# A mixture-of-experts block on one core: the moving operand of the expert matmuls read in strides of 16-byte lines

## The chip, the cores and the metric

The kernel runs on one core of a Trainium2 chip. Its time is the device time of one execution, in microseconds (us). Two executions of the kernel before were timed, at 1880.53 and 1886.04 us; their median is 1883.28 us. One further execution was profiled, and everything below about where the time goes is read from that one.

## The reference, cut to what matters

The input has 8 groups of 1024 tokens, 256 values each. A gated recurrence runs first (three 256 x 256 projections, a sigmoid, a scan over the tokens), then a layer norm, a top-2 router over 8 experts, and the experts:

```python
# per expert E (8), group G (8), slot C (256), width M = 256, hidden H = 1368
expert_inputs = einsum('GSEC,GSM->EGCM', dispatch, x)
layer_w0 = einsum('EGCM,EMH->EGCH', expert_inputs, w0_kernel)
layer_w1 = einsum('EGCM,EMH->EGCH', expert_inputs, w1_kernel)
hidden = gelu(layer_w0) * layer_w1
expert_outputs = einsum('EGCH,EHM->EGCM', hidden, wo_kernel)
out = einsum('EGCM,GSEC->GSM', expert_outputs, combine)
```

Everything is float32. Each of the 8 experts has 8 x 256 = 2048 slots, and the hidden width 1368 is ten chunks of 128 and one of 88.

## The kernel before

Two parts follow each other. The first (the functions under `pipeline`) takes the 8 groups through the projections, the recurrence and the router, and scatters token rows into slots in HBM. The second (the functions under `experts`) is what the change touches; it loops over 8 experts, over 4 tiles `t` of 512 slots and over 11 chunks `hc` of hidden units.

For one chunk of one tile TensorE does two things:

- `up_chunk` (matmul at L1186): for w0 and w1 it multiplies 128 weight columns (the stationary operand, a slice of `whi` or `wlo`) by the tile's tokens (the moving operand, 512 columns of `xThi` or `xTlo`). Float32 accuracy comes from splitting each operand into a high and a low part and adding three of the four products (`PARTS`), over two halves `k` of the width: 2 x 3 x 2 = 12 matmuls of 512 columns, into the PSUM banks `up[hc % 2]`.
- `down_chunk` (matmul at L1202), two chunks behind: 128 tokens of the hidden values (`hhi` or `hlo`, now the stationary operand) by the 256 columns of wo for this chunk (columns 512 to 767 of `whi[:, hc]` or `wlo[:, hc]`, the moving operand), for four groups `j` of tokens and three products: 12 matmuls of 256 columns, into the banks `yb`, which collect over all 11 chunks.

Every matmul has a stationary operand of its own, so each is preceded by a weight load (LDWEIGHTS, engine PEld in the profile), which runs while the matmul before it streams its columns. The order on TensorE is written out by hand: up 0, up 1, up 2, down 0, up 3, down 1, ..., up 10, down 8, down 9, down 10. After up 6 stand eight 128 x 128 transposes (L1125) that prepare the next tile's tokens. The last chunk has 88 hidden units: before, its up matmuls load 88 stationary columns (`n`) and write 88 partitions, and its down matmuls have 88 rows.

ScalarE applies the gelu and rounds to the high part (L732, L738), VectorE multiplies and takes the low part (L1011, L1014). In tile 3 of an expert ScalarE and VectorE also split the next expert's weights (L723 and L1000), chunk by chunk as the down matmuls have finished with the old ones.

In SBUF, one float32 takes 4 bytes of each partition, so 4 columns are one line of 16 bytes, and 128 columns (512 bytes) are 32 lines. The buffers are laid out with paddings to multiples of 128 columns plus or minus one line: `xThi` and `xTlo` begin at a multiple of 128 columns, row `hc` of `whi` is 772 columns long and so begins `hc` lines behind such a multiple, and the same row of `wlo` one line earlier than that.

```python
whi = sb("whi", [P, HC, WROW], F32R)[:, :, 0:WCOL]
sb("between", [P, -(HC * WROW + 4) % P])
wlo = sb("wlo", [P, HC, WROW], F32R)[:, :, 0:WCOL]
```

Of the kernel before, what the change touches and what calls it, by code (L numbers as in the profile page):

```python
# [26 lines left out]
P = 128  # L27
# [42 lines left out]
class Chain:  # L70
# [14 lines left out]

    def end(self):
        assert self.n == self.per, (self.n, self.per)


def build(nc, x_in, w_qkva, gamma_in, router_in, w0_in, w1_in, wo_in, out):  # L90
    G, S, D = x_in.shape
    E, _, H = w0_in.shape
    CAP = (2 * S // E + 3) // 4 * 4
    KD = D // P
# [4 lines left out]
    HC = -(-H // P)  # L99
    HLAST = H - (HC - 1) * P  # L100
# [8 lines left out]
    WCOL = 2 * KD * P + D  # L109
# [10 lines left out]
    with ExitStack() as ctx:  # L120
        def sb(name, shape, dt=F32):
            return ctx.enter_context(nc.sbuf_tensor(name, shape, dt))

        def sem(name):
            return ctx.enter_context(nc.semaphore(name))
# [7 lines left out]
        xThi = sb("xThi", [P, 2, KD, T], F32R)  # L133
        xTlo = sb("xTlo", [P, 2, KD, T], F32R)
# [8 lines left out]
# [3 lines that stand above are left out]
# [64 lines left out]
        up = [bank[2:4], bank[5:7]]  # L210
        yb = [bank[4], bank[7]]
# [33 lines left out]
        back = sem("back")  # L245
# [786 lines left out]
        def _(pe):  # L1032
# [80 lines left out]
            for k in range(KD):  # L1113
                for c in range(NCH):
                    last = pe.transpose(bank[2 + 2 * k + c // 4][:, (c % 4) * P:(c % 4 + 1) * P],
                                        wraw[:, c, k * P:(k + 1) * P], ident[:, :])
# [52 lines left out]

            def up_chunk(e, t, hc):  # L1170

                n = P if hc < HC - 1 else HLAST
                c = HC * t + hc
                if t == 0:

                    wait(pe, w_split, e, HC, hc + 1)
                if hc == 0:
                    wait(pe, fx_lo, e, KD * FT, KD * (t + 1))

                user = c - 2 if hc >= 2 else c - hc - HC + max(q for q in range(HC) if q % 2 == hc)  # L1180
                wait(pe, mul_done, e, HC * FT, user + 1 + FREE_MUL)
                for w, done in ((0, up0), (1, up1)):
                    for m, (wp, xp) in enumerate(PARTS):
                        for k in range(KD):
                            at = (w * KD + k) * P
                            last = pe.matmul(up[hc % 2][w][0:n, :], (whi, wlo)[wp][:, hc, at:at + n],  # L1186
                                             (xThi, xTlo)[xp][:, t % 2, k, :],
                                             start=m == 0 and k == 0, stop=m == 2 and k == KD - 1)
                    last.then_inc(done, 1)

            def down_chunk(e, t, hc):

                n = P if hc < HC - 1 else HLAST
                wait(pe, h_lo, e, HC * FT, HC * t + hc + 1)
                if hc == 0:

                    wait(pe, y_read, e, FT * FJ, FJ * t + FJ)
                    pe.wait_ge(routed, G)
                for j in range(FJ):
                    for m, (wp, xp) in enumerate(PARTS):  # L1200

                        last = pe.matmul(yb[j // 2][:, (j % 2) * D:(j % 2 + 1) * D],  # L1202
                                         (hhi, hlo)[xp][0:n, hc % 3, j * P:(j + 1) * P],
                                         (whi, wlo)[wp][0:n, hc, 2 * KD * P:WCOL],
                                         start=hc == 0 and m == 0 and j % 2 == 0,
                                         stop=hc == HC - 1 and m == 2, skip_group_check=True)
                last.then_inc(down, 1)
# [36 lines left out]
```

## Time and profile before

| | us |
|---|---|
| median of the two timed executions | 1883.28 |
| the profiled execution | 1893.51 |
| its span, first to last instruction | 1891.6 |
| of the span, the first part, before the first expert matmul | 332 |
| from the first expert matmul to the last one's end | 1538.9 |
| TensorE busy with matmuls | 1779.5 |
| TensorE weight loads | 1531.4 |
| VectorE busy | 833.3 |
| ScalarE busy | 723.4 |

The profiled execution took 0.5% more than the median. A matmul's duration in the trace is longer than the distance to the next one's start, because matmuls are pipelined; what counts for the time is that distance from start to start, called the pitch below. The timeline merges neighbouring instructions of one kind ("x2"), so the pitch is the difference of two start times divided by the number of matmuls between them. The peak rate is one column per cycle of TensorE's 2.4 GHz clock, which would be 213.3 ns for 512 columns and 106.7 ns for 256.

### The profile page before, as it was taken

Reading aid. Unit: us, or ns where it says so; the run is one execution under the profiler, and the core shown is the slowest. Engines: PE = TensorE matmul, PEld = TensorE weight load, DVE = VectorE, ACT = ScalarE, POOL = GpSimd, SP = SyncE. Lnnn points to the kernel's source line nnn. Section 1 sums busy time; section 2 is a strip of 40 time slices with the busy share of each in tenths; the row PEclk is TensorE's granted clock in tenths of the full one; section 3 lists DMA queues with packets and bytes.
Section 4 is the critical chain, followed back from the end, with each engine's and each line's share of the span. In section 5 each row is a group of like instructions: output and inputs, shape, how many; then the busy total and the mean of one; then the engine's idle time right before and its main releaser. Section 6 shows DMA issues by size and latency. Waiting matters only on the chain.

```text
span 1891.6 us, 28176 instructions
## 1 busy us (share of the span) xinstructions
PE 1779.5 (94%) x10284; PEld 1531.4 (81%) x10284; DVE 833.3 (44%) x1672; ACT 723.4 (38%) x1242; POOL 394.7 (21%) x309
## 2 busy tenths in 40 slices
PE   5988885899999999999999999999999999999995
PEld 4776765688888888888888888888888888888884
DVE  5886764333443344334533353335333533353331
ACT  4554442233343334333433343335333533353331
POOL 3365556411111111111111111111111111111111
PEclk9988885799999999999999999999999999999998
DMA  9345423111321132113311231123112411142222
GB/s 315 116 170 191 152 96 124 57 23 23 82 54 23 23 81 55 23 23 70 66 23 23 66 70 23 23 59 77 23 23 49 87 23 23 40 95 49 75 67 56
DMA packets 113037, 129.76 MB, mean 69 GB/s; under 512 B 14552, under 2 KB 100504, under 8 KB 112792
## 3 DMA queue, kind: packets, MB, share of 16 engines
q1 hardware_dynamic: 88344, 94.21, 16.5%
q0 software_dynamic: 24576, 33.83, 10.5%
q8 instruction: 93, 1.52, 0.3%
q14 instruction: 24, 0.20, 0.0%
HBM read 68.23 MB, written 68.16 MB: 72 GB/s over the span
## 4 chain that ended last, share of the span: by engine, by line
PE 83%; DVE 4%; issue 4%; ACT 3%; POOL 3%; another core or an unknown queue 1%; DMA 1%; SPq 0%; ACTq 0%; DVEq 0%; POOLq 0%
PE bank L1186 52%; PE bank L1202 26%; POOL slots L549 2%; PE bank L1125 2%; PE bank L1050 1%; ACT xn L623 1%; DVE y L811 1%; ACT rows L639 1%; DVE st L832 1%; PE bank L1095 0%; DVE wlo L1000 0%; POOL sums L600 0%; DVE xTlo L803 0%; POOL pw L532 0%
## 5 line engine op out<-in xcount | busy, mean ns | idle before, releaser
L1011 DVE TENSOR_TENSOR y<-bank,sig 128x512 f32<-128x512 f32 (+1 forms) x352 | 243.2, 691 | 637.3 <-PE bank L1186 625.5
L600 POOL DMA_INDIRECT sums<-xring x128 | 207.5, 1621 | 1309.6 <-ACT xring L752 1196.3
L1186 PE MATMUL bank<-xThi,whi 128*128 128x512 f32 (+1 forms) x1408 | 445.8, 398 | 13.7 <-DVE wlo L1000 10.0
L1186 PE MATMUL bank<-xTlo,whi 128*128 128x512 f32 (+1 forms) x1408 | 443.9, 396 | 1.4 <-issue 1.4
L1186 PE MATMUL bank<-xThi,wlo 128*128 128x512 f32 (+1 forms) x1408 | 443.3, 396 | 1.5 <-issue 1.5
L738 ACT ACTIVATE hhi<-y 128x512 fp32r<-128x512 f32 (+1 forms) x352 | 222.5, 632 | 554.2 <-DVE y L1011 550.0
L1202 PE MATMUL bank<-whi,hhi 128*128 128x256 f32 (+1 forms) x1408 | 397.7, 282 | 0.0
L1202 PE MATMUL bank<-wlo,hhi 128*128 128x256 f32 (+1 forms) x1408 | 395.3, 281 | 1.5 <-issue 1.5
L1202 PE MATMUL bank<-whi,hlo 128*128 128x256 f32 (+1 forms) x1408 | 395.1, 281 | 1.5 <-issue 1.5
L1014 DVE TENSOR_TENSOR hlo<-y,hhi 128x512 fp32r<-128x512 f32 (+1 forms) x352 | 243.7, 692 | 246.3 <-ACT hhi L738 246.3
L732 ACT ACTIVATE sig<-bank 128x512 f32<-128x512 f32 (+1 forms) x352 | 210.4, 598 | 317.9 <-PE bank L1186 310.7
L1186 PEld LDWEIGHTS bank<-xThi,wlo 128*128 128x128 f32 (+1 forms) x1408 | 262.2, 186 | 70.1 <-issue 3.0
L1186 PEld LDWEIGHTS bank<-xTlo,whi 128*128 128x128 f32 (+1 forms) x1408 | 262.0, 186 | 68.7 <-issue 1.5
L1186 PEld LDWEIGHTS bank<-xThi,whi 128*128 128x128 f32 (+1 forms) x1408 | 243.6, 187 | 56.1 <-issue 17.6
L1202 PEld LDWEIGHTS bank<-whi,hhi 128*128 128x128 f32 (+1 forms) x1408 | 265.0, 188 | 12.8 <-issue 0.4
L1202 PEld LDWEIGHTS bank<-whi,hlo 128*128 128x128 f32 (+1 forms) x1408 | 264.9, 188 | 11.5 <-issue 0.4
L1202 PEld LDWEIGHTS bank<-wlo,hhi 128*128 128x128 f32 (+1 forms) x1408 | 265.3, 188 | 2.6 <-issue 2.6
L549 POOL DMA_INDIRECT slots<-rows,sloti x128 | 124.8, 975 | 87.0 <-DVE rows L918 45.4
L1000 DVE TENSOR_TENSOR wlo<-stage,whi 128x768 fp32r<-128x768 f32 x77 | 72.5, 956 | 33.7 <-ACT whi L723 31.8
L1050 PE MATMUL bank<-xThi,wThi 128*128 128x512 f32 x192 | 71.5, 456 | 14.1 <-DVE y L811 11.3
L752 ACT ACTIVATE xring<-bank,gslot 128x256 f32<-128x256 f32 x128 | 50.0, 473 | 73.8 <-PE bank L1202 73.8
L723 ACT ACTIVATE whi<-stage 128x768 fp32r<-128x768 f32 x77 | 63.7, 836 | 32.6 <-DMA stage<-in_L_ffn_wo_kernel 29.0
(109 smaller groups left out, 1096.7 us busy)
## 6 DMA issues: line engine op xcount, KB each, us to landing
stage<-in_L_ffn_w_kernel SPq DMA_DIRECT2D x160, 128.0 KB, 2.8
slots<-fill SPq DMA_DIRECT2D x32, 520.0 KB
xring<-slots SPq DMA_DIRECT2D x32, 520.0 KB
stage<-in_L_ffn_wo_kernel SPq DMA_DIRECT2D x80, 128.0 KB, 2.9
xring<-in_L_attn_x SPq DMA_DIRECT2D x16, 512.0 KB
sums<-xring SPq DMA_DIRECT2D x16, 512.0 KB
slots<-rows,sloti POOLq DMA_INDIRECT x128
sums<-xring POOLq DMA_INDIRECT x128, 3.8
```

The costliest lines, as they stand in the source:

```text
L549: pool.indirect_dma_start(slots[:, :], bass.IndirectOffsetOnAxis(sloti[:, g.parity, k, t:t + 1], 0), rows[:, g.parity, t, :], None).then_i ...
L600: pool.indirect_dma_start(sums[:, :], bass.IndirectOffsetOnAxis(idx, 0), ysb[:, t % 2, j, :], None, compute_op=ALU.add).then_inc(added, 16)
L723: act.activation(whi[:, hc, :], stage[:, hc % STAGES, :], ACT.Copy).then_inc(w_hi, 1)
L732: act.activation(gel[0:n, hc % 2, :], up[hc % 2][0][0:n, :], ACT.Gelu_apprx_tanh).then_inc(gelu_done, 1)
L738: act.activation(hhi[0:n, hc % 3, :], hf[0:n, hc % 2, :], ACT.Copy).then_inc(h_hi, 1)
L752: act.activation(ysb[:, t % 2, j, :], yb[j // 2][:, (j % 2) * D:(j % 2 + 1) * D], ACT.Copy, scale=gslot[:, t % 2, j:j + 1]).then_inc(y_rea ...
L1000: dve.tensor_tensor(wlo[:, hc, :], stage[:, hc % STAGES, :], whi[:, hc, :].bitcast(F32), ALU.subtract).then_inc(w_split, 1)
L1011: dve.tensor_tensor(hf[0:n, hc % 2, :], up[hc % 2][1][0:n, :], gel[0:n, hc % 2, :], ALU.mult).then_inc(mul_done, 1)
L1014: dve.tensor_tensor(hlo[0:n, hc % 3, :], hf[0:n, hc % 2, :], hhi[0:n, hc % 3, :].bitcast(F32), ALU.subtract).then_inc(h_lo, 1)
L1050: last = pe.matmul(dst[:, :], (wThi, wTlo)[wp][:, k, cols], (xThi, xTlo)[xp][:, h, k, :], start=m == 0 and k == 0, stop=m == 2 and k == KD ...
L1186: last = pe.matmul(up[hc % 2][w][0:n, :], (whi, wlo)[wp][:, hc, at:at + n], (xThi, xTlo)[xp][:, t % 2, k, :], start=m == 0 and k == 0, sto ...
L1202: last = pe.matmul(yb[j // 2][:, (j % 2) * D:(j % 2 + 1) * D], (hhi, hlo)[xp][0:n, hc % 3, j * P:(j + 1) * P], (whi, wlo)[wp][0:n, hc, 2 * ...
```

## The change

All expert matmuls read the columns of their moving operand in another order and write the columns of their result in the same other order, so that every result still lands where it did. The columns are taken in lines of four. With "every4" a matmul reads lines 0, 4, 8, ... to the end, then 1, 5, 9, ..., then 2, 6, ..., then 3, 7, ...; "every8" and "every16" do the same in steps of 8 and 16 lines; "every4 back" goes through each of its four passes from the end; "swapped" reads lines 1, 0, 3, 2, 5, 4, .... Which order is used depends on the tile `t` alone. In the up matmuls of the last chunk all 128 stationary columns are loaded and all 128 partitions are written; the 40 further ones hold columns that nobody reads the result of.

```diff
+def reordered(ap, order):
+
+    if order == "every4":
+        return ap.rearrange("p (i q c) -> p q i c", q=4, c=4)
+    if order == "every4 back":
+        return ap.rearrange("p (i q c) -> p q i c", q=4, c=4)[:, :, ::-1, :]
+    if order == "every8":
+        return ap.rearrange("p (i q c) -> p q i c", q=8, c=4)
+    if order == "every16":
+        return ap.rearrange("p (i q c) -> p q i c", q=16, c=4)
+    assert order == "swapped"
+    return ap.rearrange("p (i q c) -> p i q c", q=2, c=4)[:, :, ::-1, :]
+
+
+UP_ORDER = ("every4", "every8", "every4 back", "every16")
+DOWN_ORDER = ("every4", "every8", "every4 back", "swapped")
...
             def up_chunk(e, t, hc):
 
-                n = P if hc < HC - 1 else HLAST
...
-                            last = pe.matmul(up[hc % 2][w][0:n, :], (whi, wlo)[wp][:, hc, at:at + n],
-                                             (xThi, xTlo)[xp][:, t % 2, k, :],
+                            last = pe.matmul(reordered(up[hc % 2][w][:, :], UP_ORDER[t]),
+                                             (whi, wlo)[wp][:, hc, at:at + P],
+                                             reordered((xThi, xTlo)[xp][:, t % 2, k, :], UP_ORDER[t]),
                                              start=m == 0 and k == 0, stop=m == 2 and k == KD - 1)
...
-                        last = pe.matmul(yb[j // 2][:, (j % 2) * D:(j % 2 + 1) * D],
+                        last = pe.matmul(reordered(yb[j // 2][:, (j % 2) * D:(j % 2 + 1) * D], DOWN_ORDER[t]),
                                          (hhi, hlo)[xp][0:n, hc % 3, j * P:(j + 1) * P],
-                                         (whi, wlo)[wp][0:n, hc, 2 * KD * P:WCOL],
+                                         reordered((whi, wlo)[wp][0:n, hc, 2 * KD * P:WCOL], DOWN_ORDER[t]),
```

No instruction is added, removed or moved on any engine; only the patterns of TensorE's matmuls change. On TensorE, at the end of the last up chunk of tile 0 of an expert and the start of the down chunk behind it, the kernel before has these rows (the shape is partitions x columns of the result):

```order
L1186 MATMUL bank<-xThi,whi 88x512 x2
L1186 MATMUL bank<-xTlo,whi 88x512 x2
L1186 MATMUL bank<-xThi,wlo 88x512 x2
L1202 MATMUL bank<-whi,hhi 128x256
L1202 MATMUL bank<-whi,hlo 128x256
L1202 MATMUL bank<-wlo,hhi 128x256
```

At the same place the changed kernel has the same six, as 4 passes of 32 lines of 4 columns and 4 passes of 16 lines:

```order
L1203 MATMUL bank<-xThi,whi 128x4x32x4 x2
L1203 MATMUL bank<-xTlo,whi 128x4x32x4 x2
L1203 MATMUL bank<-xThi,wlo 128x4x32x4 x2
L1220 MATMUL bank<-whi,hhi 128x4x16x4
L1220 MATMUL bank<-whi,hlo 128x4x16x4
L1220 MATMUL bank<-wlo,hhi 128x4x16x4
```

In tile 3 the two groups of matmuls have these shapes, 16 passes of 8 lines, and 32 pairs of lines:

```order
L1203 MATMUL bank<-xThi,whi 128x16x8x4 x2
L1220 MATMUL bank<-whi,hhi 128x32x2x4
```

The number of columns in a matmul is 512 or 256 in all of them, as before.

## Rows read from the trace of the kernel before

**Rows 1.** The page: span, busy time, the chain that ended last.

```profile
span 1891.6 us, 28176 instructions
...
PE 1779.5 (94%) x10284; PEld 1531.4 (81%) x10284; DVE 833.3 (44%) x1672; ACT 723.4 (38%) x1242; POOL 394.7 (21%) x309
...
PE bank L1186 52%; PE bank L1202 26%; POOL slots L549 2%; PE bank L1125 2%; PE bank L1050 1%; ACT xn L623 1%; DVE y L811 1%; ACT rows L639 1%; DVE st L832 1%; PE bank L1095 0%; DVE wlo L1000 0%; POOL sums L600 0%; DVE xTlo L803 0%; POOL pw L532 0%
```

**Rows 2.** Waits of TensorE from 430 us to the end.

```profile
PE bank L1186 <- DVE wlo L1000: 10.0, 5, 2.1
PE bank L1186 <- issue: 2.6, 4, 1.8
```

**Rows 3.** Windows: tiles 1, 2, 3 of expert 5; stretch, length, busy, PEclk, DMA share, GB/s.

```profile
1351.13:1398.19 47.06, 47.06 (x274) 40.84 (x273) 16.88 (x27) 15.86 (x28) 6.58 (x4) 1.00 0.14 23
1398.19:1445.25 47.06, 47.06 (x274) 40.84 (x273) 16.88 (x27) 15.86 (x28) 6.61 (x4) 1.00 0.14 23
1445.25:1492.23 46.98, 46.98 (x273) 40.76 (x272) 25.05 (x38) 22.98 (x38) 6.60 (x4) 1.00 0.51 113
```

**Rows 4.** Timeline of TensorE, up chunks 0 and 1 of a tile; start, length in us.

```profile
1400.03 0.62 PE L1186 MATMUL bank<-xTlo,whi 128*128 128x512 f32 x2
...
1403.20 0.62 PE L1186 MATMUL bank<-xThi,wlo 128*128 128x512 f32 x2
```

**Rows 5.** Timeline of TensorE, same tile: transposes, down 4, down 5, up 8.

```profile
1423.32 1.03 PE L1125 MATMUL bank<-ident,xring 128*128 128x128 f32 x8
1424.11 0.36 PE L1202 MATMUL bank<-whi,hhi 128*128 128x256 f32 x1
1424.31 0.28 PE L1202 MATMUL bank<-whi,hlo 128*128 128x256 f32 x1
...
1425.44 0.28 PE L1202 MATMUL bank<-wlo,hhi 128*128 128x256 f32 x1
...
1428.35 0.28 PE L1202 MATMUL bank<-whi,hhi 128*128 128x256 f32 x1
...
1429.64 0.28 PE L1202 MATMUL bank<-wlo,hhi 128*128 128x256 f32 x1
1429.76 0.63 PE L1186 MATMUL bank<-xThi,whi 128*128 128x512 f32 x2
...
1432.11 0.62 PE L1186 MATMUL bank<-xThi,wlo 128*128 128x512 f32 x2
```

**Rows 6.** Timeline of TensorE at the start of expert 2, granted clock at half.

```profile
730.34 1.05 PE L1186 MATMUL bank<-xTlo,whi 128*128 128x512 f32 x2
731.20 1.05 PE L1186 MATMUL bank<-xThi,wlo 128*128 128x512 f32 x2
732.05 0.91 PE L1186 MATMUL bank<-xThi,whi 128*128 128x512 f32 x2
```

**Rows 7.** Groups of weight loads by shape: xcount, busy us, mean ns.

```profile
L1186 PEld LDWEIGHTS bank<-xTlo,whi 128*128 128x128 f32 x1280 | 242.2, 189 | 58.5 <-issue 1.5
L1202 PEld LDWEIGHTS bank<-whi,hhi 128*128 128x128 f32 x1280 | 241.0, 188 | 12.8 <-issue 0.4
L1186 PEld LDWEIGHTS bank<-xTlo,whi 128*88 128x88 f32 x128 | 19.7, 154 | 10.2
```

**Rows 8.** Timeline of TensorE in the first part: 16 router matmuls of 8 columns.

```profile
143.31 1.95 PE L1095 MATMUL bank<-router,x2nT 128*128 128x8 f32 x16 [0.36 <-ACT x2nT L648]
```

## The prediction

> **What bounds the kernel now.** The page comes first: TensorE is busy for 94% of the span, and the chain that ended last lies for 78% on two lines, L1186 (up) and L1202 (down) [rows 1]. From 430 us to the end TensorE waits 12.6 us in all [rows 2]. So the time of the second part is a number of matmuls times their pitch, and nothing else.
>
> The windows of whole tiles say what that is. Tiles 1 and 2 of expert 5 take 47.06 us each; tile 3, in which VectorE works 25.05 us instead of 16.88 and the DMA engines are busy for 0.51 instead of 0.14, takes 46.98 us up to the start of its last matmul [rows 3]. The reader is to see two things: every tile takes the same time, and what the other engines and the DMAs do beside it has no influence on TensorE's rate.
>
> A tile has 132 up and 132 down matmuls and eight transposes. The transposes begin at 1423.32 and the first down matmul behind them at 1424.11; that matmul then takes 0.20 us to the next start where 0.11 is usual [rows 5]. That is 0.79 + 0.09 = 0.88 us. The rest, 47.06 - 0.88 = 46.18 us over 132 pairs, is 349.8 ns for one up and one down matmul. At peak rate a pair is 213.3 + 106.7 = 320.0 ns. So 29.8 ns of each pair, 8.5%, are stalls while the granted clock is 1.00. Over 4224 pairs (8 experts x 4 tiles x 132) they are 126 us, 6.7% of the time. This is all that another reading order can win.
>
> What the stalls are is read from the timeline, by the start times:
>
> - Up matmuls in chunks 0 and 1: 14 matmuls from 1400.03 to 1403.20, 226.4 ns each [rows 4]. Up matmuls in chunk 8: 10 from 1429.76 to 1432.11, 235 ns [rows 5]. Same moving operand, same shape; what differs is the weight row, which lies `hc` lines behind a 512-byte boundary.
> - Down matmuls in chunk 4: 10 from 1424.31 to 1425.44, 113 ns; in chunk 5: 11 from 1428.35 to 1429.64, 117.3 ns [rows 5].
> - At the half clock the pitch is (732.05 - 730.34) / 4 = 427.5 ns, which is 512 columns at 1.2 GHz with nothing on top [rows 6]. The stalls exist only when the columns are asked for at full speed.
>
> So the pitch depends on where the stationary and moving reads stand relative to each other, and not on data or on other engines. I read this as two reads of TensorE, the moving columns and the next weight load, getting in each other's way in SBUF. The weight load takes 34 or 35 ns less for 40 columns less (154 against 188 and 189, [rows 7]), so it reads one column in 0.85 ns, at half the speed of the moving columns at most; it moves in the same direction, and a moving read that starts behind it catches it up and stays near it for several lines.
>
> **The change part by part.**
>
> 1. *Order of the moving columns, 8448 matmuls.* No matmul has more columns or more instructions. Reading in steps of 4, 8 or 16 lines, the moving read crosses the weight load's place quickly and often instead of slowly and once. The number of meetings need not fall (on average both visit each place equally often), but the long ones go. I take as the price after the change the best pitch that the trace shows for stretches without long meetings: 226.4 and 113 ns, 339.4 together [rows 4, 5]. The gain is 349.8 - 339.4 = 10.4 ns per pair, over 4224 pairs 44 us; rounded down for the few matmuls at half clock and for those already at the best pitch at a tile's start, which stay there at best, 42 us. This is the term that the forecast rests on, and the trace does not show the operation itself. Its bounds: at the best no stall is left in the up matmuls (213.3) and the down matmuls run into the weight load, which by itself gives a pitch of (1.95 - 0.27) / 15 = 112 ns where 16 matmuls of 8 columns follow each other ([rows 8]; 0.27 is about the last one's length): 325.3 ns per pair, a gain of 24.5 ns or 103 us. At the worst every jump to another line costs what the slower reader needs for a column, 0.85 ns [rows 7]: 128 lines and 64 lines, 192 x 0.85 = 163 ns per pair, a loss of 689 us. The best pitch seen lies nearest to the present rows, so I take that, 42 us.
>
> 2. *The same order on the output in PSUM.* Every line of four is still written in one run of 16 bytes. No row shows a result written in steps by a wide matmul, so this has the bounds of the term above and is part of it. I take nothing.
>    The Trainium skill speaks against me here: "PSUM — Partial Sum Buffer", section "Specifications (TRN2)", says that any non-contiguous access pattern slows matmuls significantly. "Advanced Engine Details and Errata", section "PSUM Cachelines", gives the reason in a weaker form, that every two consecutive elements should be contiguous, which runs of four satisfy. No row of this trace shows either. By the first the change would be a loss, by the second free on this side.
>
> 3. *128 instead of 88 stationary columns in the last chunk, 384 matmuls.* The weight load grows from 154 to 189 ns [rows 7] and is hidden behind an up matmul of 226 ns or more; the 40 further partitions are written at the same time as the 88. Cost 0. Were the cover gone, 384 x 0.035 = 13 us; below nothing it can hardly go, since a weight load that ends sooner is no help to a matmul that lasts longer.
>
> 4. *What comes late next.* In tile 3 each weight row of the next expert is split once the old one is free, and TensorE waits for it at the start of an expert, 2.1 us at the longest [rows 2]. This chain starts at the last down matmuls and not at the tile's start, so it stays as long as it is. A tile of 45.7 us still leaves VectorE (25.05 us) and ScalarE (22.98 us) half idle [rows 3]. Nothing new binds, at most 1 us per expert, which I leave out.
>
> The sum for the profiled execution: 1893.5 - 42 = 1851.5 us. It ran 0.5% above the median; on the median of the runs, 1883.3 - 42 = 1841 us.
>
> **The rivals.**
>
> *No change that counts, 1883 us (1850 to 1915).* The meetings become shorter, but there are more of them, and the moving read loses as much as before, or the stalls belong to the stream itself. For it: even the best stretches carry 13 ns above the peak for 512 columns and 6 for 256, in proportion to the columns although a weight load covers only half of the longer matmul, so a part is not a meeting at all. Also, chunks 0 and 1 would lose their good place and give back 24 of 132 matmuls x 7 ns x 32 tiles = 5 us. Against it: the differences of up to 9 ns by weight row [rows 4, 5] can only come from the pair of reads. That the change does not do what it says (that the array reads ahead in address order whatever the pattern) would end here too.
>
> *More than forecast, 1780 us.* All stalls are long meetings, and the pair goes to 325.3 ns: 1883.3 - 103. For it: the full rate at half clock [rows 6]. Against it: no stretch of the trace at full clock is that fast.
>
> *Slower: lines far apart cost the reader time.* If consecutive lines have to come from different places to be read at full speed, steps of 16 lines come back to the same place at once. With 0.85 ns per line in the up matmuls of tile 3 alone, 8 x 132 x 128 x 0.85 ns = 115 us, 1998 us; with half speed (427 instead of 233 ns, [rows 6]) in the up matmuls of tiles 1 and 3, 2112 x 194 ns = 410 us. It decides as soon as the average pair loses 9 ns (38 us), which is 0.05 ns per line. For it: reading is already at its limit, as the 8.5% show. Against it: half clock's exact rate shows no cost by line at that speed, and tiles 0 and 2 step by only 4 lines.
> The rule of the Trainium skill nearest to it is in "SBUF — State Buffer", section "Door 1: The DMA port swizzle": SBUF has lines of 16 bytes, at least two hits in a line are needed for full bandwidth, and each access to a new line pays. By that rule the old and the new order pay alike, four hits a line and the same number of lines, and the change would come out at no change.
>
> **How the numbers follow.** The forecast's mechanism, with the better case in it, has 0.45: 1841 us, own range 1775 to 1850. No change that counts has 0.30. Slower has 0.25, spread widely because only its bounds are known: about 0.10 for one tile's order losing a little (1920 to 1960), 0.15 for losses of 100 us and more. A measurement of this kernel can tell about 2% from no change, 38 us, and the forecast of 42 us is just over it. The range must reach into both: 1765 to 1960 leaves out some 0.03 below and 0.15 above.
>
> **What would show it right or wrong.** In the changed kernel's trace the pitch can be read per tile, and each tile is one order: up at 226 and down at 113 in all chunks, hardly different from chunk to chunk, would be the forecast, with tiles of 45.7 us against 47.06. Tiles that differ strongly from each other show that the stride matters by itself: tile 3 (steps of 16 in the up matmuls) far longer than tiles 0 and 2 is the slower rival. Tiles of 47 us with every chunk alike are the rival of no change. Up matmuls below 220 ns would be the larger gain, and pitches that still depend on the weight row would show that meetings have not gone. The last up chunk should have the pitch of its neighbours. Wrong altogether would be a change in TensorE's waits or in the first part, which the edit does not touch.

## The result, and the profile after

The changed kernel takes 1940.36 us (median of two executions, 1938.32 to 1942.39), the kernel before 1883.28 us: a ratio of 1.030, 95% interval 1.022 to 1.038, 57 us slower. The profiled execution took 1942.39 us.

The page of the changed kernel, the lines that answer to [rows 1]:

```profile
span 1940.3 us, 28176 instructions
...
PE 1834.7 (95%) x10284; PEld 1550.2 (80%) x10284; DVE 835.7 (43%) x1672; ACT 732.3 (38%) x1242; POOL 392.2 (20%) x309
...
PE bank L1203 54%; PE bank L1220 26%; POOL slots L567 2%; PE bank L1143 1%; PE bank L1068 1%; DVE y L829 1%; ACT xn L641 1%; PE bank L1113 0%; DVE st L850 0%; DVE st L794 0%; ACT rows L657 0%; DVE xTlo L821 0%; DVE wlo L1018 0%; POOL sums L618 0%
```

TensorE's waits from 430 us to the end, as in [rows 2]:

```profile
PE bank L1203 <- DVE wlo L1018: 10.8, 5, 2.3
PE bank L1203 <- issue: 2.5, 4, 1.8
```

TensorE is busy for 55 us longer, with the same number of instructions, and its waits are what they were (13.3 us against 12.6). The loss is all pitch. Each tile of an expert has its own order, so one window for each tile takes it apart. The windows of the four tiles of expert 7 in the kernel before (for tile 3 up to the start of its last matmul; columns as in [rows 3]):

```profile
1683.54:1730.65 47.11, 47.11 (x275) 40.88 (x274) 18.64 (x29) 16.59 (x29) 6.21 (x4) 1.00 0.14 23
1730.65:1777.71 47.06, 47.06 (x275) 40.84 (x274) 16.85 (x27) 15.86 (x28) 6.21 (x4) 1.00 0.26 68
1777.71:1824.77 47.06, 47.06 (x275) 40.84 (x274) 16.86 (x27) 15.81 (x28) 6.21 (x4) 1.00 0.26 68
1824.77:1870.76 45.99, 45.99 (x264) 39.80 (x263) 15.22 (x22) 14.89 (x26) 6.21 (x4) 1.00 0.23 58
```

And in the changed kernel:

```profile
1725.14:1771.10 45.96, 45.96 (x274) 40.82 (x273) 18.61 (x29) 16.53 (x29) 6.21 (x4) 1.00 0.15 24
1771.10:1820.43 49.33, 49.33 (x274) 42.21 (x273) 16.87 (x27) 16.01 (x28) 6.22 (x4) 1.00 0.25 65
1820.43:1867.36 46.93, 46.93 (x275) 41.04 (x273) 16.86 (x27) 15.82 (x28) 6.21 (x4) 1.00 0.26 68
1867.36:1919.46 52.10, 52.10 (x265) 40.77 (x263) 15.23 (x22) 15.49 (x26) 6.58 (x4) 1.00 0.21 51
```

Tile 0 gains 1.15 us, tile 1 loses 2.27, tile 2 gains 0.13, tile 3 loses 6.11: together 7.10 us per expert, and 8 x 7.10 = 57 us. Between the two profiled executions the expert part is 55 us longer (1593.7 us against 1538.9) and the first part 6 us shorter (326.2 us against 332.2). The edit does not touch the first part; in the other kernels' traces, where it is the same code, it takes 301 to 330 us, so the 6 us are no effect of the change. The four tiles were four experiments in one kernel. The mean pitches (all start-to-start distances of one kind in a tile at the full clock, over the experts, without waits) are:

| order | up, ns | down, ns |
|---|---|---|
| straight (kernel before) | 232 | 118 |
| every4 (tile 0) | 226 | 115.5 |
| every8 (tile 1) | 245 | 122.4 |
| every4 back (tile 2) | 232 | 116.8 |
| every16 up, swapped down (tile 3) | 277 | 119.2 |

In the timeline the reader sees the same by dividing: in chunk 5 of tile 3 of expert 5, ten matmuls from the first to the last of these rows are 2.77 us, 277 ns each, where the up matmuls of [rows 5] had 235.

```profile
1494.55 0.72 PE L1203 MATMUL bank<-xThi,whi 128*128 128x512 f32 x2
...
1497.32 0.73 PE L1203 MATMUL bank<-xThi,wlo 128*128 128x512 f32 x2
```

### The profile page after: what moved, and what is told of

It reads as the page before. It is cut to its first block, busy times and chain, and to the rows that moved or that the text cites. A ratio compares the mean times of both kernels' runs of the same rounds, so it can differ in the third digit from the quotient of the medians.

```text
span 1940.3 us, 28176 instructions
## 1 busy us (share of the span) xinstructions
PE 1834.7 (95%) x10284; PEld 1550.2 (80%) x10284; DVE 835.7 (43%) x1672; ACT 732.3 (38%) x1242; POOL 392.2 (20%) x309
## 4 chain that ended last, share of the span: by engine, by line
PE 84%; DVE 5%; issue 4%; POOL 3%; ACT 2%; another core or an unknown queue 1%; DMA 1%; SPq 0%; DVEq 0%; ACTq 0%; POOLq 0%
PE bank L1203 54%; PE bank L1220 26%; POOL slots L567 2%; PE bank L1143 1%; PE bank L1068 1%; DVE y L829 1%; ACT xn L641 1%; PE bank L1113 0%; DVE st L850 0%; DVE st L794 0%; ACT rows L657 0%; DVE xTlo L821 0%; DVE wlo L1018 0%; POOL sums L618 0%
## 5 line engine op out<-in xcount | busy, mean ns | idle before, releaser
L1203 PE MATMUL bank<-xThi,whi 128*128 128x512 f32 x1408 | 464.3, 411 | 16.2 <-DVE wlo L1018 10.8
L1203 PE MATMUL bank<-xThi,wlo 128*128 128x512 f32 x1408 | 463.3, 411 | 0.5 <-issue 0.4
L1203 PE MATMUL bank<-xTlo,whi 128*128 128x512 f32 x1408 | 463.5, 411 | 0.0
L1203 PEld LDWEIGHTS bank<-xThi,wlo 128*128 128x128 f32 x1408 | 269.0, 191 | 80.2 <-issue 1.2
L1203 PEld LDWEIGHTS bank<-xTlo,whi 128*128 128x128 f32 x1408 | 268.7, 191 | 79.2 <-issue 0.4
L1203 PEld LDWEIGHTS bank<-xThi,whi 128*128 128x128 f32 x1408 | 248.2, 191 | 66.4 <-issue 19.7
```

The lines of the kernel that those rows point to most:

```text
L1203: last = pe.matmul(reordered(up[hc % 2][w][:, :], UP_ORDER[t]), (whi, wlo)[wp][:, hc, at:at + P], reordered((xThi, xTlo)[xp][:, t % 2, k, ...
```

## The experiments

The kernels of the experiments have the orders of reading and writing in separate tables; "straight" leaves an operand as it was. What a table holds is given for tiles 0 to 3. All of them load 128 stationary columns in the last chunk, as the changed kernel does, but for narrow_load. Up and down pitches below are means over a tile as above. Where no interval is given, a time is that of a single execution; all_every4 has four and tile3_up_straight ten.

### read_only and write_only: is it the reading or the writing?

```diff
 read_only
+UP_READ   = ("every4", "every8", "every4 back", "every16")
+DOWN_READ = ("every4", "every8", "every4 back", "swapped")
+UP_WRITE, DOWN_WRITE: straight
 write_only
+UP_READ, DOWN_READ: straight
+UP_WRITE   = ("every4", "every8", "every4 back", "every16")
+DOWN_WRITE = ("every4", "every8", "every4 back", "swapped")
```

> The moving columns are read in the changed order, but the result's columns are written straight, so the result's columns come out permuted. The changed kernel's tiles showed four pitches for an up matmul: about 226 ns in tile 0 (steps of 4 lines), 245 in tile 1 (8), 232 in tile 2 (4, backwards), 277 in tile 3 (16), where straight order has 232; down matmuls 115.5, 122.4, 116.8 and 119.2 ns where straight order has 118. Theory 1, the reading of the moving columns in SBUF makes the difference: the same pitches by tile, tiles 1 and 2 take 49.3 and 46.9 us, and the time is about 1940 us. Theory 2, the writing of the result in PSUM makes it: all tiles take 47.06 us as before and the time is about 1883 us. If both share in it, tile 1 lies between 47.1 and 49.3 us.

> The moving columns are read straight, and the result's columns are written in the changed order (permuted columns again). Theory 1 (reading in SBUF): all tiles 47.06 us, about 1883 us. Theory 2 (writing in PSUM): tiles 1 and 2 take 49.3 and 46.9 us, tile 3's up matmuls have 277 ns, about 1940 us.

read_only took 1944.57 us, write_only 1890.21, with the kernel before at 1888.19 on the same chip (median of seven executions, 1881 to 1896). The windows of expert 7 in read_only:

```profile
1727.24:1773.20 45.96, 45.96 (x274) 40.82 (x273) 18.61 (x29) 16.53 (x29) 6.21 (x4) 1.00 0.14 24
1773.20:1822.54 49.34, 49.34 (x275) 42.22 (x274) 16.89 (x27) 16.02 (x28) 6.22 (x4) 1.00 0.24 65
1822.54:1869.46 46.92, 46.92 (x274) 41.04 (x273) 16.84 (x27) 15.83 (x28) 6.21 (x4) 1.00 0.26 68
1869.46:1921.56 52.10, 52.10 (x265) 40.77 (x263) 15.22 (x22) 15.48 (x26) 6.58 (x4) 1.00 0.20 51
```

And in write_only:

```profile
1727.67:1774.75 47.08, 47.08 (x275) 41.22 (x274) 16.84 (x27) 15.86 (x28) 6.24 (x4) 1.00 0.25 68
...
1821.83:1867.84 46.01, 46.01 (x264) 40.20 (x263) 15.21 (x22) 14.89 (x26) 6.21 (x4) 1.00 0.23 58
```

The read-only kernel has the changed kernel's tiles to 0.01 us, the write-only kernel the tiles of before to 0.02 us. The whole effect is the reading of the moving columns in SBUF. The order in which PSUM is written costs nothing that shows (the 0.02 us are there in last128 below too, which writes straight).

### last128: the second part of the change by itself

```diff
-                n = P if hc < HC - 1 else HLAST
-   pe.matmul(up[hc % 2][w][0:n, :], (whi, wlo)[wp][:, hc, at:at + n], ...)
+   pe.matmul(up[hc % 2][w][:, :], (whi, wlo)[wp][:, hc, at:at + P], ...)
```

> The kernel before with one part of the change: 128 stationary columns loaded and 128 partitions written in the last chunk's up matmuls. Theory: the longer weight load is hidden, tiles of 47.06 us and 1883 us within 0.3%. Rival: a longer weight load meets the moving columns for longer, and the last chunk's up matmuls take a few ns more, 384 x 5 ns = 2 us; if it were not hidden at all, 13 us.

1887.91 us against 1888.19. Tile 1 of expert 7:

```profile
1725.22:1772.30 47.08, 47.08 (x275) 41.22 (x274) 16.85 (x27) 15.88 (x28) 6.22 (x4) 1.00 0.26 68
```

Weight loads are busy for 0.38 us more, the tile is 0.02 us longer (the last chunk's up pitch goes from 232 to 234 ns). Over 32 tiles that is under 1 us.

### all_every4: the good tile's order everywhere

```diff
-UP_ORDER = ("every4", "every8", "every4 back", "every16")
-DOWN_ORDER = ("every4", "every8", "every4 back", "swapped")
+UP_ORDER = ("every4", "every4", "every4", "every4")
+DOWN_ORDER = ("every4", "every4", "every4", "every4")
```

> Steps of 4 lines in all four tiles, read and written, for up and down matmuls. If the cost of an order belongs to the order and not to the tile it stands in, all tiles take what tile 0 takes in the changed kernel, 45.96 us in expert 7 against 47.1 before, and the time is 1883 - 32 x 1.1 = 1848 us (ratio 0.981 to the kernel before). If tile 0's gain came from its place (what stood in the pipelines before it), tiles 1 to 3 stay near 47 us and the time is near 1875 us.

1860.64 us against 1888.19 on the same chip, a ratio of 0.985, interval 0.981 to 0.988. Tiles 0 and 1 of expert 7:

```profile
1658.45:1704.41 45.96, 45.96 (x275) 40.81 (x273) 18.71 (x30) 16.52 (x29) 6.21 (x4) 1.00 0.14 24
1704.41:1750.38 45.97, 45.97 (x275) 40.82 (x274) 16.83 (x27) 15.86 (x28) 6.21 (x4) 1.00 0.27 70
```

The price belongs to the order and not to the tile's place. This kernel beats both others, by 28 us against the kernel before; that is 1.5%, less than the 2% that count as a change here. The tiles were to give 32 x 1.1 = 35 us, and the interval (22 to 35 us) just takes that in. The trace shows where the rest went. After TensorE's wait at the start of experts 1 to 6 the granted clock is at half for a stretch of 3.4 us all six times, in the kernel before only twice. In expert 4, in this kernel and in the kernel before:

```profile
1097.70:1101.10 3.40, 3.40 (x10) 2.66 (x9) 0.00 (x0) 1.28 (x2) 2.13 (x2) 0.50 0.12 8
...
1112.33:1115.73 3.40, 3.11 (x13) 2.29 (x14) 0.30 (x1) 2.15 (x3) 1.55 (x1) 1.00 0.03 5
```

Each such stretch makes tile 0 take 47.7 us instead of 45.96, so the four more of them are 7 us. The longest wait is 2.5 us here and 2.1 in the kernel before; why the clock fell more often here is not shown.

The mean of 226 ns also hides something. In steps of 4 the pitch still changes with the weight row: over the experts, tile 1's up matmuls of chunk 3 have 220.1 ns and those of chunk 1 have 230.8. In expert 5, ten matmuls of chunk 1 and ten of chunk 3:

```profile
1335.55 0.62 PE L1208 MATMUL bank<-xThi,whi 128*128 128x512 f32 x2
...
1337.85 0.63 PE L1208 MATMUL bank<-xThi,wlo 128*128 128x512 f32 x2
...
1342.40 0.60 PE L1208 MATMUL bank<-xThi,whi 128*128 128x512 f32 x2
...
1344.61 0.61 PE L1208 MATMUL bank<-xThi,wlo 128*128 128x512 f32 x2
```

### tile3_up_straight: undo the most expensive cell

```diff
-UP_ORDER = ("every4", "every8", "every4 back", "every16")
+UP_ORDER = ("every4", "every8", "every4 back", "straight")
```

> The changed kernel with one cell undone: the up matmuls of tile 3 read in straight order instead of steps of 16 lines, all else as changed. If the loss is the sum of its tiles' pitches, this cell is worth 8 x 132 x (277.3 - 232) ns = 48 us, and the time is 1940 - 48 = 1892 us, a ratio of 1.005 to the kernel before (tile 1's loss of 8 x 2.27 = 18 us against the gains of tiles 0, 2 and tile 3's down matmuls unchanged). If part of the cost would move elsewhere (a wait on the other engines hidden before), it stays above 1900 us.

1898.57 us against 1889.21, a ratio of 1.006, interval 1.004 to 1.009. The last tile is back at the length of before, tile 1 is not:

```profile
1729.83:1779.30 49.47, 49.47 (x274) 42.24 (x273) 16.86 (x27) 16.02 (x28) 6.21 (x4) 1.00 0.24 65
...
1826.23:1872.21 45.98, 45.98 (x264) 40.17 (x263) 15.22 (x22) 14.89 (x26) 6.21 (x4) 1.00 0.23 58
```

Of the 57 us, 48 are the 1056 up matmuls that step by 16 lines: that is their pitch, the last tile gives 8 x 6.12 = 49 us, and the two kernels' ratios to the kernel before, 1.030 and 1.006, lie 46 us apart. Within the noise the loss is a plain sum of pitches.

### narrow_load: is it a meeting with the weight load?

This was the mechanism of my prediction. The kernel loads a quarter of the stationary columns and leaves 96 of 128 hidden units of every chunk out of the up products. The down matmuls keep their full weight loads.

```diff
+UP_READ = UP_WRITE = DOWN_READ = DOWN_WRITE = ("straight", "every4", "every8", "every16")
-   pe.matmul(up[hc % 2][w][:, :],    (whi, wlo)[wp][:, hc, at:at + P], ...)
+   pe.matmul(up[hc % 2][w][0:32, :], (whi, wlo)[wp][:, hc, at:at + 32], ...)
```

> Up matmuls with only 32 of 128 stationary columns (one quarter of the weight load; 96 of the hidden units of each chunk are left out), moving columns in straight order in tile 0, steps of 4, 8 and 16 lines in tiles 1, 2, 3; down matmuls as they were, in the same four orders. Seen so far with 128 stationary columns: 232, 226, 245, 277 ns, that is 19, 13, 31 and 64 ns above the 213.3 ns of the peak rate. Theory M, meetings of the moving read with the weight load: with a quarter of the load a quarter of the excess stays, 218, 217, 221 and 229 ns; the tiles differ by at most 12 ns. Theory S, the moving read waits for itself when it comes back to the same place in SBUF: the excess stays, 232, 226, 245, 277 ns. Down matmuls in steps of 16 (not seen yet): by either theory above 119 ns, near 130.

This run and the next two were on a chip on which the kernel before took 1853.62 us. The pitches are the same there where an order was run on both chips (down matmuls in straight order 118.4 ns against 118, up matmuls in steps of 16 lines 276.5 against 277.3); what is shorter is the time up to the first of them, 301 to 304 us in these three kernels against 332 in the kernel before and 326 in the changed one. So these runs are read by pitch and not by total.

The group of weight loads in narrow_load:

```profile
L1208 PEld LDWEIGHTS bank<-xTlo,whi 128*32 128x32 f32 x1408 | 155.6, 110 | 192.0 <-issue 62.0
```

And the windows of its tiles 0, 1, 2 of expert 7:

```profile
1702.91:1749.98 47.07, 47.07 (x274) 31.38 (x272) 18.30 (x29) 16.63 (x29) 6.21 (x4) 1.00 0.14 23
1749.98:1795.63 45.65, 45.65 (x274) 30.78 (x272) 16.85 (x27) 15.78 (x28) 6.21 (x4) 1.00 0.27 70
1795.63:1845.20 49.57, 49.57 (x274) 32.38 (x272) 16.84 (x27) 15.89 (x28) 6.21 (x4) 1.00 0.25 64
```

A weight load went from 189 to 110 ns, and the up pitches are 231.9, 222.7, 245.7 and 276.7 ns. Meetings would have left a quarter of each excess; nearly all of it stays, and only in steps of 4 do 3.5 of 13 ns go. Theory M falls as the cause of the stalls; most of them belong to the moving read itself.

The weight row still matters by a few ns. In straight order the chunks' means go from 229.3 to 235.2 ns (227.3 to 234.7 in the kernel before), in steps of 4 from 218.0 to 227.7. In the best chunk of tile 1, chunk 6, eight matmuls from the first to the last of these rows take 216 ns each, almost the full rate:

```profile
1374.11 0.59 PE L1208 MATMUL bank<-xTlo,whi 128*32 128x512 f32 x2
...
1375.84 0.60 PE L1208 MATMUL bank<-xThi,wlo 128*32 128x512 f32 x2
```

### more_strides and longer_runs: what about the order costs?

```diff
 more_strides
+UP_READ   = UP_WRITE   = ("every2", "every32", "every64", "swapped")
+DOWN_READ = DOWN_WRITE = ("every2", "every16", "every32", "straight back")
 longer_runs (runs of 8 columns every 2nd, 4th, 8th; runs of 16 columns every 4th)
+UP_READ = UP_WRITE = DOWN_READ = DOWN_WRITE = ("pairs2", "pairs4", "pairs8", "quads4")
```

> Orders by tile: up matmuls in steps of 2, 32, 64 lines and pairs swapped; down matmuls in steps of 2, 16, 32 lines and straight backwards. Each pass over the columns ends with a jump back: a step of q has q passes. Theory P, each pass costs about 4 ns (steps of 8 and 16 have 8 and 16 passes, 31 and 64 ns above peak): steps of 32 give 213 + 128 = 341 ns, steps of 64 give 470 ns. Theory B, SBUF has a number of banks by line address and what costs is coming back to a bank that a weight load is using or that was just used: the pitch stops rising where the step is the number of banks, so 64 like 32, and if there are 32 banks the step of 32 is the worst by far. Steps of 2 lie between straight and 4 by both: 226 to 232 ns up, 115 to 118 ns down. Swapped pairs: like straight, 232.

> Runs of 2 lines (8 columns) taken every 2nd, 4th and 8th run in tiles 0 to 2, and runs of 4 lines (16 columns) every 4th run in tile 3, for up and down matmuls. The distance between runs is 4, 8, 16 and 16 lines. If the distance in lines decides, the up pitches are those of steps of 4, 8 and 16: 226, 245, 277 ns and again 277. If the number of passes decides (2, 4, 8, 4): near 230, 226, 245, 226 ns. If the number of jumps decides (64, 64, 64, 32 per matmul against 128), each excess over straight halves, and tile 3's is a quarter.

more_strides: up 232.6 (every2), 267.8 (every32), 252.6 (every64), 232.8 (swapped); down 117.5 (every2), 135.5 (every16), 127.5 (every32), 118.8 (straight back). The price rises to steps of 16 and falls again, so it is not the number of passes (theory P said 341 and 470 ns). Theory B missed too: the worst step is 16, and 32 and 64 are not alike. The timeline, chunk 5 of tiles 1 and 2, ten matmuls each, 269 and 253 ns:

```profile
1387.68 0.70 PE L1208 MATMUL bank<-xThi,whi 128*128 128x512 f32 x2
...
1390.37 0.71 PE L1208 MATMUL bank<-xThi,wlo 128*128 128x512 f32 x2
...
1440.59 0.66 PE L1208 MATMUL bank<-xThi,whi 128*128 128x512 f32 x2
...
1443.12 0.68 PE L1208 MATMUL bank<-xThi,wlo 128*128 128x512 f32 x2
```

longer_runs: up 232.7, 230.2, 247.1, 237.7; down 118.0, 116.4, 124.3, 118.8. Runs of two lines 16 lines apart cost 15 ns over straight where single lines cost 45, and runs of four 6: nearest to the third reading (the number of jumps decides), with less left than it said. For runs of two lines 8 lines apart even the excess over straight is gone (230.2 where single lines have 245).

### two_streams and odd_steps: which distance is bad?

Both leave some columns out and read others twice; the number per matmul is unchanged.

```diff
+    if isinstance(order, tuple):
+        (s1, n1), (s2, n2) = order
+        return bass.AP(tensor=ap.tensor, offset=ap.offset,
+                       ap=[list(ap.ap[0]), [4 * s1, n1], [4 * s2, n2], [1, 4]])
 two_streams: lines i, i + d, i + 1, i + 1 + d, ...; up every16, d = 8, 16, 32; down d = 4, 8, 16, 32
 odd_steps: steps of 3, 5, 7, 12 lines (4, 8, 8, 16 passes)
```

> Up matmuls read two streams in turn, line i and then line i + d, for i from 0 to 63 (some columns twice, some never: the product is another one, the number of columns is 512 as ever): d = 8, 16, 32 in tiles 1, 2, 3; tile 0 reads in steps of 16 lines. Down matmuls the same with d = 4, 8, 16, 32 in tiles 0 to 3. Known: steps of 64 lines, which is d = 64, have 252.6 ns (39 above the peak), steps of 16 have 277. Theory 16, places in SBUF that repeat every 16 lines (256 bytes), and a line costs more when the line just read is of the same place: d = 16 and 32 cost what 64 costs, 252 ns up and near 127 ns down, and d = 8 (and 4) is like straight order, 232 and 118. Theory 32, the place repeats every 32 lines: only d = 32 is like 64, and d = 16 is like straight. Theory P, it is the number of passes: with one pass all of them are like straight order. At the half clock, which the starts of the first experts have, tile 0's up matmuls in steps of 16 should keep 427 ns if stalls come only where a line is asked for every 1.67 ns; if a line of a repeated place has a cost of its own in any case, they would be at 450 ns and more.

> Steps of 3, 5, 7 and 12 lines in tiles 0 to 3 (some columns left out, the number read is 512 and 256 as ever). Theory 16: odd steps come back to the same of 16 places only after 16 lines, as straight order does, and steps of 12 after 4 lines, as steps of 4 do: 3, 5 and 7 near 232 ns and 118 ns, 12 near 226 and 115. If the distance itself costs (a jump of 12 lines being longer than one of 8), 12 lies between steps of 8 and 16, 245 to 277 ns, and 3, 5, 7 rise in order. Rival: places are passed best in odd steps, and 3, 5, 7 are faster than any seen, 220 ns and less.

two_streams: up 242.6 (d = 8), 252.5 (16), 252.6 (32), and 252.6 for d = 64 (steps of 64 above); down 121.6, 122.5, 127.5, 127.5 (d = 4, 8, 16, 32). With one pass only, d = 16 costs what 32 and 64 cost: theory 16 holds for these, theories 32 and P fall. d = 8 was to be like straight and is not: it costs 10 ns in the up matmuls, and d = 8 and d = 4 cost about 4 in the down matmuls.

At the half clock tile 0 of the same kernel, in steps of 16 lines, has (748.54 - 745.98) / 6 = 427 ns:

```profile
745.14 1.04 PE L1212 MATMUL bank<-xTlo,whi 128*128 128x512 f32 x2
745.98 1.05 PE L1212 MATMUL bank<-xThi,wlo 128*128 128x512 f32 x2
746.83 1.05 PE L1212 MATMUL bank<-xThi,whi 128*128 128x512 f32 x2
...
748.54 0.73 PE L1212 MATMUL bank<-xThi,wlo 128*128 128x512 f32 x2
749.10 0.73 PE L1212 MATMUL bank<-xThi,whi 128*128 128x512 f32 x2
```

That is 512 columns at 1.2 GHz with nothing on top, as straight order had in [rows 6]; right behind it, at the full clock, the pair from 748.54 to 749.10 takes 280 ns a matmul. Steps of 16 lines, the worst order in the changed kernel, cost nothing when a line is wanted every 3.33 ns.

odd_steps: up 227.7 (3), 272.4 (5), 233.4 (7), 232.7 (12); down 116.1, 116.6, 123.2, 117.4. Steps of 3 are nearly as good as steps of 4. Steps of 12 are not as bad as a long jump would make them, but not as good as steps of 4. Steps of 5 are at 273 ns in the up matmuls, in every chunk, and not in the down matmuls; steps of 7 are like straight in the up matmuls and 5 ns above it in the down matmuls. None of the theories has that, and it stays open.

### bf16_lines and short_runs: lines per time

bf16_lines takes bfloat16 constants for both operands of the up matmuls, 8 columns a line, and leaves the up products out. Every weight load of its up matmuls then reads the same block of constants, and takes 97 ns instead of 189. short_runs takes 2 columns a line for the reads it names, and in its first three tiles writes runs of 2 columns (the columns come out permuted).

```diff
 bf16_lines, moving operand of the up matmuls
+UP_READ = ("whole lines", "whole lines every16", "half lines", "half lines every16")
 short_runs ("runs c of q": runs of c columns, every q-th)
+UP_WRITE = ("runs 2 of 4", "runs 2 of 2", "runs 2 of 16", "straight")
+UP_READ   = ("straight", "straight", "straight", "runs 2 of 2")
+DOWN_READ = ("runs 2 of 2", "runs 2 of 8", "straight", "straight")
```

> Up matmuls with bfloat16 operands from a buffer of constants, so that a line of 16 bytes holds 8 columns (the up products are left out; their results are constants). Tile 0: whole lines in straight order; tile 1: whole lines in steps of 16; tile 2: the first 4 columns of each line, straight; tile 3: the first 4 columns of each line, steps of 16. Theory L, what is short is lines per time (a whole line of float32 lasts 1.67 ns, one of bfloat16 3.33 ns): tiles 0 and 1 at 214 to 216 ns, tiles 2 and 3 as float32, 232 and 277 ns. Theory F, the stalls belong to float32 columns (4 bytes per column and cycle) whatever the lines: all four tiles at 216 ns. If steps of 16 cost by themselves: tiles 1 and 3 above 230 ns.

> Runs of 2 columns (8 bytes). Written in PSUM (read straight, up matmuls): every 4th pair, every 2nd pair, every 16th pair in tiles 0, 1, 2. Read from SBUF: up matmuls of tile 3 every 2nd pair, down matmuls every 2nd pair in tile 0 and every 8th in tile 1. If PSUM minds any column that does not follow the last one, tiles 0 to 2 rise above 232 ns (runs of four cost nothing in write_only); if it takes 8 bytes at a time, they stay at 232. For reading: a line of 16 bytes now gives 2 columns and not 4, so twice as many lines per time are asked for. If a line is fetched for each run, an up matmul of tile 3 reads 256 lines at no less than 1.67 ns, 427 ns, and a down matmul 213 ns and more; if 8 bytes are what is fetched, they stay near 232 and 118 ns (every 2nd pair) and above (every 8th pair, 4 lines apart).

Chunk 5 of tiles 0 to 3 of expert 5 in bf16_lines, twelve matmuls merged in each row, which end 0.12 and 0.07 us later where only half of each line is used:

```profile
1283.70 2.76 PE L1227 MATMUL bank<-narrow 128*128 128x512 bf16 x12
...
1328.78 2.76 PE L1227 MATMUL bank<-narrow 128*128 128x512 bf16 x12
...
1374.43 2.88 PE L1227 MATMUL bank<-narrow 128*128 128x512 bf16 x12
...
1420.57 2.83 PE L1227 MATMUL bank<-narrow 128*128 128x512 bf16 x12
```

By single starts the pitches are 216, 216, 226 and 222 ns, each constant to 2 ns but for the first one of a chunk, which is 10 to 13 ns longer. With whole lines, half as many per time as in float32, straight order and steps of 16 cost the same, 3 ns above the peak. With a line for every 4 columns straight order is at 226 ns, the float32 kernel's best, in every chunk. So theory L holds for straight order, up to the 5 ns by which float32's mean of 232 lies above; what took these away (one weight row for all, the shorter weight load or the type) was not separated. For steps of 16 theory L does not hold (222 and not 277): their extra price was seen in float32 alone.

In short_runs, up matmuls of tile 3 and down matmuls of tile 0 have twice the lines. Chunk 5 of each, ten matmuls and eleven:

```profile
1785.47 1.07 PE L1211 MATMUL bank<-xThi,whi 128*128 128x512 f32 x2
...
1789.98 1.10 PE L1211 MATMUL bank<-xThi,wlo 128*128 128x512 f32 x2
...
1621.45 0.39 PE L1228 MATMUL bank<-whi,hhi 128*128 128x256 f32 x1
...
1623.96 0.41 PE L1228 MATMUL bank<-wlo,hhi 128*128 128x256 f32 x1
```

That is 451 and 228 ns (means 453.1 and 228.1). 453.1 ns over 256 lines is 1.77 ns a line, 228.1 over 128 is 1.78, and the best pitches of the kernel before, 226.4 over 128 lines and 113 over 64 [rows 4, 5], are 1.77 too. In straight order, then, the moving read gets a line every 1.77 ns at its best, and the full clock wants one every 1.67. So each run of 2 columns costs a line, and the theory of 8 bytes at a time falls. The 1.77 ns are no limit for every order: the down matmuls of tile 1, whose reads lie 4 lines apart, have twice the lines too and take 220 ns, 1.72 ns a line, and the rows of narrow_load above, in steps of 4 lines, have 216 / 128 = 1.69. The written runs of 2 columns are at 234, 233 and 232 ns in tiles 0 to 2 at the full clock.

## Why the prediction was wrong, step by step

I forecast 1841 us and a gain of 42; measured are 1940 us and a loss of 57.

- *What bounds the kernel.* Right. Everything that changed is the pitch of L1186 and L1202, the waits did not move, and the stalls are 29.8 ns a pair.
- *What the stalls are.* This is the step that failed: "two reads of TensorE, the moving columns and the next weight load, getting in each other's way in SBUF". I had it from the pitch changing with the weight row, and from nothing else. With a quarter of the weight load the excess stays (narrow_load), and in which direction a weight load reads, on which the long meetings hung, no run shows. The trace of before already spoke against it, and the prediction says so under its first rival: the stalls grow with the columns, 13 ns and 6, although a weight load covers only half of the longer matmul. I weighed that too little. What the runs show in its place is that the moving read's own lines set the price: how many are wanted per time (216 ns with half as many in bfloat16, 226 with as many, 453 with twice as many, nothing above the peak at the half clock) and how far apart consecutive ones lie (277 ns in steps of 16, 226 in steps of 4). Straight order gets a line every 1.77 ns at best, which gives 226.7 ns and 113.3 ns and is 20 of the 29.8 ns of a pair. Why it is 1.77 and not 1.67 stays open. So does the rest of straight order's 232 and 118, which changes with the weight row: it is the smaller part, and a meeting with the weight load is not excluded for it.
- *Part 1, one price for all orders.* Wrong with it: the price is the order's. Steps of 4 come out near the forecast's price (226.1 and 115.5 ns against 226.4 and 113), and all_every4 gives 28 us of the 42, but that is luck in good part: the pitch was to be hardly different from chunk to chunk, and it goes from 220.1 to 230.8 ns, which was the prediction's own sign that the meetings have not gone. Steps of 8 and 16 do the opposite. Over 8 x 132 pairs the four tiles are -9, +18, -1 and +49 us.
- *Part 2, PSUM, taken as nothing.* Right, shown by write_only. The Trainium skill's sentence in "PSUM — Partial Sum Buffer", "Specifications (TRN2)", that any non-contiguous pattern slows matmuls significantly, does not hold for runs of 4 columns or of 2. The form in "Advanced Engine Details and Errata", "PSUM Cachelines", two consecutive elements, agrees with short_runs; the same section repeats the stronger sentence too.
- *Part 3, 128 stationary columns.* Right: under 1 us (last128).
- *Part 4, what comes late next.* Right: the wait for the split weights is 10.8 us against 10.0.
- *The slower rival* had the right mechanism, "steps of 16 lines come back to the same place at once", and the wrong size. It priced each line of tile 3 at the weight load's 0.85 ns, 115 us; measured are 48 us. It had 0.25, of which 0.10 for a loss of this size. That 1940 us lies inside the range of 1765 to 1960 is owed to this rival and not to the forecast's mechanism.

The price of a line that follows one of the same place can be worked out. Call two lines of the same place if their distance is a multiple of 16 (256 bytes). Then, over the 1.77 ns a line of straight order's best:

| order | lines following one of the same place | above 226.7 or 113.3, ns | per such line, ns |
|---|---|---|---|
| every16, up | 112 of 128 | 277.3 - 226.7 = 50.6 | 0.45 |
| every32, up | 96 | 41.1 | 0.43 |
| every64, up | 64 | 25.9 | 0.40 |
| two streams, d = 16, up | 64 | 25.8 | 0.40 |
| every16, down | 48 of 64 | 22.2 | 0.46 |
| every32 and d = 16, down | 32 | 14.2 | 0.44 |

Six orders, nearly one number: 0.40 to 0.46 ns, about one cycle of 2.4 GHz. It hangs on the 1.77 taken off first; by the differences between these orders a line more costs 0.48 to 0.59 ns ((277.3 - 267.8) / 16 and so on). That the places are banks of the memory is my reading; what is shown, for float32 at the full clock, is that distances of 16, 32 and 64 lines cost alike. Coming back after one other line costs less: 0.16 ns a line in steps of 8 (245 ns), and runs of two lines 16 lines apart, which do the same, have 247. After three others it cost nothing in steps of 4, but steps of 12 and runs of four lines 16 apart come back as soon and have 233 and 238 ns.

Not settled: what sets the 1.77 ns of straight order, which steps of 4 go below (220.1 ns in a chunk, 216 with narrow loads); why d = 4 and d = 8 cost something, although they come back to the same place only after many lines; why steps of 5 cost 273 ns in the longer matmuls alone; why half lines of bfloat16 in steps of 16 pay no extra price; and why backwards in steps of 4 is 6 ns worse than forwards. A rule of 16 places alone gives none of these.

## What to carry to other kernels

A float32 matmul at the full clock asks SBUF for a 16-byte line of the moving operand every 1.67 ns, and in straight order these runs got one every 1.77 at best: the order in which the moving operand is read is then on the critical path. Let float32 columns come in whole lines, and keep consecutive lines from being a multiple of 256 bytes apart (a view that takes 4 columns of every 64 or 128 has just that distance); steps of 4 lines were the best of the orders tried here, 1.5% of the whole kernel. A mean that hits a forecast is no proof of its mechanism: look at the spread that the mechanism promised, too. And where one constant explains a stall and a second observation does not fit, price the change by both explanations: a change that treats four cases alike only under one of them is the test.

## What the runs showed that I had not expected

- The order in which a matmul writes PSUM is free to 2 ns in 232, down to runs of 2 columns 16 pairs apart.
- Two float32 columns from each line halve TensorE's rate (453 ns for 512 columns). The Trainium skill, "SBUF — State Buffer", "Door 1: The DMA port swizzle", says that two hits in a line give full bandwidth; for float32 at the full clock two were not enough, and four in straight order still leave 6%.
- bfloat16 columns with whole lines run at 216 ns for 512 in straight order and in steps of 16 lines alike, with a weight load before every one of them. The Trainium skill's formula in "TensorE: Matmul & The Clock Gate", "Back-to-back issue gap", 512 / 2.4 + 2.5, agrees for this type. The section calls it the gap of a matmul by itself and gives about 131 ns for 512 columns in a stream of weight loads and matmuls; the stream here has 216, and the measurement decides. For float32 no order's mean reached 216: the lowest was 222.7 ns, in narrow_load's steps of 4, with single chunks at 218.
- On the chip on which the kernel before took 1853.62 us, 1.6% less, TensorE's pitches are the same. Most of the difference seems to lie ahead of the first expert matmul, which stands 20 to 30 us earlier in the three kernels traced there; the kernel before was not traced on that chip.
